# Reordered opening of the second attention of a four-layer kernel

## The chip, the cores and the metric

The kernel runs on one core of a Trainium2 chip. The metric is the device time of one execution in microseconds (us); the median of three executions of the kernel before is 891.05 us (890.66 to 892.91). A difference of 0.3% is 2.7 us.

## What is computed

The program is a chain of four layers; each has a gated cross-attention block and a gated feed-forward block. x and ctx are 8 x 128 x 256, taken as 1024 rows of 256 numbers. The change lies in the attention of the second layer ("attention 2" here): 16 heads of 16 numbers, queries, keys and values rounded to 8-bit steps, softmax, weights rounded to 255 steps:

```python
q = (x @ Wq + bq).reshape(1, B * N, H, hd)          # x is layer-normalised
kv = (cond @ Wkv + bkv).reshape(1, -1, 2, H, hd)
k, v = (kv[:, :, 0], kv[:, :, 1])
...
q = _fq_sym(q, axis=-1)
k = _fq_sym(k, axis=-1)
v = _fq_sym(v, axis=2)
attn = jnp.einsum('bhqd,bhkd->bhqk', q, k)
attn = jax.nn.softmax(attn.astype(jnp.float32), axis=-1)
attn = _fq_unsigned(attn, axis=-1)
out = jnp.einsum('bhqk,bhkd->bhqd', attn, v)
```

## The kernel before

Each engine runs one program, written out by hand in order; engines meet only at semaphores. A wait holds up everything behind it on its engine. The 1024 rows are 8 tiles of 128. Keys and values of attention 2 depend on ctx alone and are projected and rounded during the feed-forward block ahead of it, so that at the opening the rounded keys ka2 lie ready. The opening then goes like this:

- TensorE (PE) turns the rounded values (16 bf16 transposes, line 1222, into banks 0 and 1). ScalarE (ACT) copies them to v2 (two copies, line 1320).
- VectorE (DVE) finishes the residual sum (line 1026, from banks 4 to 7) and the layer norm, in two halves of four tiles: variance (line 159, semaphore var_ready), square root on ACT (`root`, line 1316, semaphore std_ready, in ACT's order behind the copies of v2), four short steps (lines 166 to 169), then the normalised rows xn tile by tile (line 171). PE turns them (line 214, f32), ACT copies them to xnT (`evacuate_T`, line 204).
- `project(half)` (line 1203) multiplies four tiles of xnT by wq2: 16 f32 matmuls of 128x256, two tiles to a bank. DVE's chain on the queries of a half goes from `take2` (line 1370, one instruction for a bank) over the scales to the rounded queries qa2, whose last instruction is line 1424 (semaphore qa2_ready).
- `turn_pairs` (line 1214) turns keys and queries, by pairs of heads: pairs 0 to 7 are keys, 8 to 15 queries. A pair is 8 bf16 transposes, one for each tile, into one of banks 4 to 7 in turn, so pair n waits for the copy of pair n - 4. ACT copies a key pair whole (line 1309, 128x1024) and the lower 64 rows of a query pair (line 1311, 64x1024); DVE copies the upper 64 rows of each query pair (line 1429) and the lower ones of pair 12 (line 1431).
- PE's order is: values, ln_tensor(2) with project(0) between the two halves, key pairs 0 to 3, project(1), key pairs 4 to 7, then a wait for both halves of qa2, then the query pairs, then a wait for the last copy.
- The loop of attention 2 follows: 128 steps n, one for each head and tile. PE makes the scores (line 1242, two matmuls of 128x512, three slots of two banks: n = 0 in banks 0 and 1, n = 1 in 2 and 3, n = 2 in 4 and 5), DVE takes the row maxima (`top`, line 1438), ACT the exponential (`exp`, line 1332), GpSimd rounds (line 1153), a DMA or PE turns the weights, and PE multiplies by the values seven steps later (lines 1263 and 1264). DVE too waits for the last copied pair ahead of its first `top`.

DMAs of this stretch are issued by SyncE (SP), which at the opening waits for the turned values and for the first 8 pairs (qkT2_blocks, line 1597), and then for the loop.

Of the kernel before, what the change touches and what calls it, by code (L numbers as in the profile page):

```python
# [46 lines left out]
def build(nc, A, out):  # L47
# [3 lines left out]
    def sem(name):  # L51
        if name not in sems:
            sems[name] = ctx.enter_context(nc.semaphore(name))
        return sems[name]
# [4 lines left out]
    with ctx:  # L59
# [1042 lines left out]
        def bf(i):  # L1102
            return bank[i].bitcast(BF16)
# [63 lines left out]
            sp.dma_start_transpose(rT2[n % RSLOTS2].rearrange("p (j q) -> p j q", j=NT), r2[n % RSLOTS2])\  # L1167
              .then_inc(sem(f"rT2_ready{n % RSLOTS2}"), 16)

        def low_by_vector(n):  # L1170
            return n == H2 // 2 + 4

        def pair_copied(eng, n):

            eng.wait_ge(sem("qkT2_ready"), sum(not low_by_vector(m) for m in range(n + 1)))
            if n >= H2 // 2:
                eng.wait_ge(sem("qT2_ready"), sum(1 + low_by_vector(m) for m in range(H2 // 2, n + 1)))

        def l1x_values_tensor(pe):

# [16 lines left out]
        def l1x_tensor(pe):  # L1197
# [7 lines left out]
                    if t % 2:  # L1205
                        last.then_inc(sem("qk2_done"), 1)

            def turn_pairs(numbers):

                for n in numbers:  # L1210
                    if n >= 4:
                        pair_copied(pe, n - 4)
                    for t in range(NT):
                        last = nc.tensor.transpose(bf(4 + n % 4)[:, t * P:(t + 1) * P],
                                                   (ka2 if n < H2 // 2 else qa2)[:, t, 2 * (n % 8):2 * (n % 8) + 2, :].rearrange("p a b -> p (a b)"),
                                                   identb[:])
                    last.then_inc(sem("qkT2_blocks"), 1)

            pe.wait_ge(sem("vi2_ready"), 1)
            for t in range(NT):  # L1220
                for c in range(DC):
                    last = nc.tensor.transpose(bf(t // 4)[:, (t % 4 * DC + c) * P:(t % 4 * DC + c + 1) * P],
                                               vi2[:, c, t * P:(t + 1) * P], identb[:])
                if t % 4 == 3:
                    last.then_inc(sem("v2_blocks"), 1)
            pe.wait_ge(sem("v2_ready"), 2)
            ln_tensor(pe, 2, lambda: project(0))
            pe.wait_ge(sem("ka2_ready"), 1)
            turn_pairs(range(4))
            project(1)  # L1230
            turn_pairs(range(4, H2 // 2))
            pe.wait_ge(sem("qa2_ready"), 2)
            turn_pairs(range(H2 // 2, H2))
            pe.wait_ge(sem("pads2_ready"), 32)
            pair_copied(pe, H2 - 1)

            def scores(n):
                h, t = n // NT, n % NT
                if n >= SRING2:
                    pe.wait_ge(sem("e2_ready"), n - SRING2 + 1)  # L1240
                for half in range(2):
                    last = nc.tensor.matmul(bank[2 * (n % SRING2) + half], qz2[:, h % 2, h // 2, t * P:(t + 1) * P],  # L1242
                                            kT2[:, h // 2, half * 512:(half + 1) * 512], start=True, stop=True)
                last.then_inc(sem("scores2_done"), 1)
# [55 lines left out]
                           kf2.rearrange("p t (h d) -> p (t h) d", h=H2)).then_inc(sem("ka2_high"), 1)  # L1300

        def l1x_scalar(act):
            def copy_pairs(numbers):
                for n in numbers:
                    if low_by_vector(n):
                        continue
                    act.wait_ge(sem("qkT2_blocks"), n + 1)
                    if n < H2 // 2:
                        nc.scalar.copy(kT2[:, n, :], bf(4 + n % 4)).then_inc(sem("qkT2_ready"), 1)
                    else:  # L1310
                        nc.scalar.copy(qz2[0:ROWS, 0, n % 8, :], bf(4 + n % 4)[0:ROWS]).then_inc(sem("qkT2_ready"), 1)

            def root(part):
                lo, hi = ln_parts(2)[part]
                act.wait_ge(sem("var_ready"), ln_roots(2) + part + 1)
                nc.scalar.activation(std[:, lo:hi], var_eps[:, lo:hi], ACT.Sqrt).then_inc(sem("std_ready"), 1)

            for b in range(2):
                act.wait_ge(sem("v2_blocks"), b + 1)
                nc.scalar.copy(v2[:, 4 * b:4 * b + 4, :].rearrange("p t d -> p (t d)"), bf(b)).then_inc(sem("v2_ready"), 1)  # L1320
            root(0)
            evacuate_T(act, xnT, sem("xnT_blocks"), sem("xnT_ready"), turned(2), 0)
            root(1)
            evacuate_T(act, xnT, sem("xnT_blocks"), sem("xnT_ready"), turned(2), 1)
            copy_pairs(range(H2))

            def exp(n):
                h, t = n // NT, n % NT
                act.wait_ge(sem("bias2_ready"), n + 1)
                if n >= ESLOTS2:  # L1330
                    act.wait_ge(sem("r2_ready"), n - ESLOTS2 + 1)
                nc.scalar.activation(e2[:, n % ESLOTS2, :], scores_at(n), ACT.Exp, bias=bias2[:, n:n + 1],  # L1332
                                     scale=s2[:, t * H2 + h:t * H2 + h + 1], accum_out=zs2[:, h, t:t + 1]).then_inc(sem("e2_ready"), 1)

            def copy_T(n):
# [12 lines left out]
            for half in range(2):  # L1348
                for c in range(DC):
                    act.wait_ge(sem("oT2_blocks"), 2 * half + c + 1)  # L1350
                    nc.scalar.activation(oT2[:, c, half * 512:(half + 1) * 512], bank[2 * half + c], ACT.Copy,
                                         scale=sv2[:, c:c + 1]).then_inc(sem("oT2_ready"), 1)
# [60 lines left out]
        def l1x_vector(dve, seq):  # L1413
            ln_vector(dve, seq, 2)
            for half in range(2):
# [7 lines left out]
                seq.step(round2(qf.rearrange("p t (h d) -> p (t h) d", h=H2), qa[:, :, 0:HD2]))  # L1423
                nc.vector.tensor_copy(qa[:, :, HD2:ROWS].rearrange("p n (a d) -> p n a d", a=3), bcast(qa[:, :, 0:HD2], 2, 3))\
                  .then_inc(sem("qa2_ready"), 1)
            for n in range(H2):
                if n >= H2 // 2:
                    dve.wait_ge(sem("qkT2_blocks"), n + 1)
                    nc.vector.tensor_copy(qz2[ROWS:P, 1, n % 8, :], bf(4 + n % 4)[ROWS:P]).then_inc(sem("qT2_ready"), 1)
                    if low_by_vector(n):  # L1430
                        nc.vector.tensor_copy(qz2[0:ROWS, 0, n % 8, :], bf(4 + n % 4)[0:ROWS]).then_inc(sem("qT2_ready"), 1)

            def top(n):
                h, t = n // NT, n % NT
# [27 lines left out]
                    dve.wait_ge(sem("values2_done"), n - RSLOTS2 + 1)  # L1462
                nc.vector.tensor_copy(rT2[n % RSLOTS2], bank[7].bitcast(F16)).then_inc(sem("rT2_copied"), 1)

            pair_copied(dve, H2 - 1)
            dve.wait_ge(sem("vi2_ready"), 1)
            U = H2 * NT
            for n in range(U):
# [1159 lines left out]
```

## Time and profile before

| | before |
|---|---|
| median of three | 891.05 us (890.66 to 892.91) |
| profiled execution | 892.17 us |
| its span, first to last instruction | 890.4 us |
| PE busy | 714.0 us, 80% |
| DVE busy | 534.0 us, 60% |
| ACT busy | 368.7 us, 41% |
| opening: last value transposes to the first `top` | 201.4 to 237.0 us |
| loop: first to last `top` | 237.0 to about 414 us |

All positions are microseconds from the start of the span. About 1.8 us of the time lie outside the span. In a row of the timeline the first number is the start, the second the length of the run of instructions merged into the row (x16 are sixteen of them), and the square bracket is the time for which the engine stood idle ahead of it and what ended that. PEclk is the granted clock of TensorE as a share of 2.4 GHz; it has two levels, 1.00 and 0.50 (1.2 GHz).

### The profile page before, as it was taken

How to read it: one execution, taken by the hardware profiler on the slowest of the kernel's cores; microseconds unless marked ns; L12 is line 12 of the kernel's file. 1: busy time of each engine (PE TensorE's matmuls, PEld its weight loads, DVE VectorE, ACT ScalarE, POOL GpSimd, SP SyncE). 2: the span in 40 equal slices, each digit the busy share in tenths (PEclk: the TensorE clock that was granted, in tenths of full speed). 3: DMA queues.
4: the chain of work that ended last, by engine and by line, in shares of the span. 5: the costliest groups of instructions: out<-in, count | busy, mean ns of one | idle time of the engine just before them, and what ended most of it. 6: DMA issues, size and time to landing. Idle time of an engine off the chain costs nothing.

```text
span 890.4 us, 14503 instructions
## 1 busy us (share of the span) xinstructions
PE 714.0 (80%) x5356; PEld 501.8 (56%) x5356; DVE 534.0 (60%) x1244; ACT 368.7 (41%) x658; POOL 303.3 (34%) x332
## 2 busy tenths in 40 slices
PE   5987798997588788887889980892966579999997
PEld 3445465676355555555657860471444446777776
DVE  3896855667899999996475545827776530000014
ACT  4002022424799999996222323342663122221210
POOL 2941130000277777775007506300320072000024
PEclk9997899997899999897898995796898569999999
DMA  7311174520199999999204848000013132515413
GB/s 239 132 59 48 26 148 159 197 74 1 23 176 193 161 198 169 183 174 161 102 25 118 146 126 279 10 0 1 0 54 137 47 87 91 207 48 182 160 39 118
DMA packets 139133, 100.08 MB, mean 112 GB/s; under 512 B 109204, under 2 KB 125238, under 8 KB 137016
## 3 DMA queue, kind: packets, MB, share of 16 engines
q1 hardware_dynamic: 132552, 81.19, 37.8%
q0 software_dynamic: 6224, 17.96, 7.6%
q8 instruction: 43, 0.70, 0.3%
q14 instruction: 26, 0.21, 0.1%
q10 hardware_dynamic: 288, 0.00, 0.0%
HBM read 61.15 MB, written 10.72 MB: 81 GB/s over the span
## 4 chain that ended last, share of the span: by engine, by line
PE 34%; issue 11%; DVE 10%; POOL 4%; ACT 4%; DMA 3%; POOLq 0%; DVEq 0%; ACTq 0%
PE psum L2342 7%; PE psum L2361 5%; PE psum L1661 3%; PE psum L1938 2%; PE psum L214 2%; ACT both L1332 2%; POOL both L568 2%; PE psum L1676 1%; DVE xnT L1438 1%; PE psum L1242 1%; PE psum L2372 1%; PE psum L1520 1%; DMA both<-both 1%; PE psum L621 1%; PE psum L635 1%
## 5 line engine op out<-in xcount | busy, mean ns | idle before, releaser
L1153 POOL TENSOR_SCALAR both<-both 128x1024 f16<-128x1024 f32 x128 | 133.7, 1045 | 162.8 <-ACT both L1332 155.0
L1438 DVE TENSOR_SCALAR_CACHE_REDUCE xnT<-psum,both 128x1024 bf16<-128x1024 f32 x128 | 157.5, 1278 | 9.1 <-PE psum L1242 8.9
L1332 ACT ACTIVATE both<-psum,both 128x1024 f32<-128x1024 f32 x128 | 153.5, 1210 | 9.2 <-DVE xnT L1438 8.7
L1242 PE MATMUL psum<-both 128*128 128x512 bf16 x256 | 84.4, 415 | 32.2 <-ACT both L1332 28.0
L2342 PE MATMUL psum<-both 128*128 128x320 f32 x256 | 73.5, 441 | 3.8 <-ACT both L556 3.8
L1263 PEld LDWEIGHTS psum<-both 128*128 128x128 f16 x1024 | 63.3, 98 | 22.7 <-DMA both<-both 8.3
L2421 ACT ACTIVATE both<-psum 128x320 f32<-128x320 f32 x64 | 27.6, 437 | 110.0 <-PE psum L2342 92.1
L1263 PE MATMUL psum<-both 128*128 128x16 f16 x1024 | 67.7, 171 | 6.4 <-DMA both<-both 2.8
L1264 PE MATMUL psum<-both,minus_base 128*128 128x16 f16 x1024 | 66.5, 170 | 0.0
L1264 PEld LDWEIGHTS psum<-both,minus_base 128*128 128x128 f16 x1024 | 58.6, 98 | 10.8 <-issue 2.7
L2342 PEld LDWEIGHTS psum<-both 128*128 128x128 f32 x256 | 48.8, 194 | 24.1 <-issue 5.3
L2361 PE MATMUL psum<-both 128*128 128x256 f32 (+1 forms) x272 | 60.5, 381 | 0.6 <-issue 0.6
L2456 DVE COPY both<-psum 128x256 f32<-128x256 f32 x14 | 5.9, 424 | 88.6 <-PE psum L2361 88.6
L2361 PEld LDWEIGHTS psum<-both 128*128 128x128 f32 (+1 forms) x272 | 50.4, 187 | 10.5 <-issue 2.5
L214 PE MATMUL psum<-ident,xn 128*128 128x128 f32 x128 | 25.9, 376 | 34.2 <-DVE xn L171 33.3
L428 POOL DMA_INDIRECT both<-moe_xn_dram,moe_token_of x31 | 30.3, 977 | 52.6 <-DVE both L400 24.6
L214 PEld LDWEIGHTS psum<-ident,xn 128*128 128x128 f32 x128 | 21.5, 194 | 38.6 <-DVE xn L171 31.5
L428 POOL DMA_INDIRECT both<-grouped_xn_dram,grouped_token_of x31 | 29.4, 949 | 30.5 <-DVE grouped_token_of L398 21.3
L1242 PEld LDWEIGHTS psum<-both 128*128 128x128 bf16 x256 | 15.3, 98 | 42.1 <-ACT both L1332 39.0
L187 ACT ACTIVATE std<-var_eps 128x4 f32<-128x4 f32 (+1 forms) x10 | 2.1, 208 | 84.0 <-DVE var_eps L159 84.0
L286 POOL TENSOR_TENSOR both<-both 128x512 f32<-128x512 f32 x32 | 32.2, 1038 | 12.9 <-ACT both L258 9.6
L1661 PE MATMUL psum<-both 128*128 x124 | 33.5, 394 | 0.3 <-ACT both L1703 0.3
(379 smaller groups left out, 1460.5 us busy)
## 6 DMA issues: line engine op xcount, KB each, us to landing
both<-in_l_experts SPq DMA_DIRECT2D x50, 384.0 KB, 3.7
both<-in_l_experts SPq DMA_DIRECT2D x16, 1024.0 KB, 5.5
grouped_y_dram<-both SPq DMA_DIRECT2D x31, 128.0 KB
ctok<-in_ctx SPq DMA_DIRECT2D x2, 1024.0 KB, 7.5
both<-kpad_dram SPq DMA_DIRECT2D x1, 2048.0 KB, 8.0
moe_xn_dram<-xn POOLq DMA_DIRECT2D x4, 512.0 KB, 3.9
both<-bp SPq DMA_DIRECT2D x2, 1024.0 KB, 12.1
moe_y_dram<-both POOLq DMA_DIRECT2D x7, 256.0 KB, 3.1
```

What stands on the lines that cost most here:

```text
L214: last = nc.tensor.transpose(bank[2 * half + c][:, t * P:(t + 1) * P], src[:, half * 4 + t, c * P:(c + 1) * P], ident[:])
L286: nc.gpsimd.tensor_tensor(kv[:, h % KVS, c, :].rearrange("p (b j i) -> p b j i", b=NT, j=HD0), bcast(rows, 3, HD0), bcast(rows, 2, HD0), A ...
L428: nc.gpsimd.indirect_dma_start(out=self.rows[:, b, :], out_offset=None, in_=self.xn_dram[:, :], in_offset=bass.IndirectOffsetOnAxis(ap=sel ...
L1153: nc.gpsimd.tensor_scalar(r2[n % RSLOTS2], e2[:, n % ESLOTS2, :], 255.0, HALF_BASE, ALU.mult, ALU.add).then_inc(sem("r2_ready"), 1)
L1242: last = nc.tensor.matmul(bank[2 * (n % SRING2) + half], qz2[:, h % 2, h // 2, t * P:(t + 1) * P], kT2[:, h // 2, half * 512:(half + 1) * ...
L1263: nc.tensor.matmul(dst, rT2[n % RSLOTS2][:, j * P:(j + 1) * P], of_block, start=(j == 0), stop=False)
L1264: last = nc.tensor.matmul(dst, minus_base[:], of_block, start=False, stop=(j == NT - 1))
L1332: nc.scalar.activation(e2[:, n % ESLOTS2, :], scores_at(n), ACT.Exp, bias=bias2[:, n:n + 1], scale=s2[:, t * H2 + h:t * H2 + h + 1], accum ...
L1438: nc.vector.tensor_scalar(scaled2[n % 2], scores_at(n), ns2[:, t * H2 + h:t * H2 + h + 1], None, ALU.mult, ALU.min, accum_out=bias2[:, n:n ...
L1661: last = nc.tensor.matmul(bank[b % 2][:, 0:2 * P].rearrange("p (j n) -> p j n", j=2), xT3[:, b % 4, c, :], w[:, :, c, :], start=(c == 0), ...
L2342: last = nc.tensor.matmul(bank[f % 4][:, 0:C7], w7[:, i, c * FF7 + f * P:c * FF7 + (f + 1) * P], moe7.rowsT[:, c, e * C7:(e + 1) * C7], st ...
L2361: last = nc.tensor.matmul(bank[4 + j][0:JT7[j][1], 0:D], h7[:, e % 2, f, JT7[j][0]:JT7[j][0] + JT7[j][1]], w7[:, e % 2, DC * FF7 + f * D:D ...
```

## The change

Nothing is computed otherwise, and no DMA is added, removed or moved. What changes is order and grain:

1. ACT: `root(0)` stands in front of the two copies of v2.
2. PE: key pairs 0 and 1 are turned right behind the values, once var_ready tells that banks 4 and 5 are free; key pairs 2 and 3 are turned between the two halves of xn, in front of `project(0)`. Pairs 4 and 5 come ahead of `project(1)`, 6 and 7 behind it. ACT's copies follow: key pair 0 ahead of the first half of xnT, 1 to 3 behind `root(1)`.
3. Queries are turned and copied by halves of four tiles: 8 pairs of 4 transposes after qa2_ready 1, then 8 pairs after qa2_ready 2. Copies are 64x512 each, 32 in all: of half 0, ACT makes the 8 lower and the first 5 upper ones, DVE the last 3 upper ones (in its order behind its whole chain on the queries); of half 1, ACT makes 6 lower ones, DVE 8 upper and 2 lower ones (pairs 2 and 5).
4. The first two scores wait for pair 0 of half 0 alone, and the wait for everything stands at n = 2. DVE's wait ahead of its first `top` is gone.

```diff
+        PAIRS2 = H2 // 2
+        def low_by_vector(half, m):
+            return half == 1 and m in (2, 5)
+        def high_by_vector(half, m):
+            return half == 1 or m >= 5
...
             pe.wait_ge(sem("vi2_ready"), 1)
...
+            pe.wait_ge(sem("ka2_ready"), 1)
+            pe.wait_ge(sem("var_ready"), ln_roots(2) + 1)
+            turn_keys(range(2))
             pe.wait_ge(sem("v2_ready"), 2)
-            ln_tensor(pe, 2, lambda: project(0))
-            pe.wait_ge(sem("ka2_ready"), 1)
-            turn_pairs(range(4))
+            ln_tensor(pe, 2, between_halves)
+            turn_keys(range(4, 6))
             project(1)
-            turn_pairs(range(4, H2 // 2))
-            pe.wait_ge(sem("qa2_ready"), 2)
-            turn_pairs(range(H2 // 2, H2))
+            turn_keys(range(6, PAIRS2))
+            turn_queries(0)
+            turn_queries(1)
             pe.wait_ge(sem("pads2_ready"), 32)
-            pair_copied(pe, H2 - 1)
             def scores(n):
+                if n < 2:
+                    q_copied(pe, 0, 0)
+                elif n == 2:
+                    q_copied(pe, 1, PAIRS2 - 1)
...
+            def between_halves():
+                turn_keys(range(2, 4))
+                project(0)
...
+            def turn_queries(half):
+                pe.wait_ge(sem("qa2_ready"), half + 1)
+                for m in range(PAIRS2):
+                    if m >= 4:
+                        q_copied(pe, half, m - 4)
+                    elif half:
+                        q_copied(pe, 0, m + 4)
+                    else:
+                        key_copied(pe, m + 4)
+                    for t in range(4):
+                        last = nc.tensor.transpose(bf(4 + m % 4)[:, t * P:(t + 1) * P],
+                                                   qa2[:, 4 * half + t, 2 * m:2 * m + 2, :].rearrange("p a b -> p (a b)"), identb[:])
+                    last.then_inc(sem("qkT2_blocks"), 1)
...
+            root(0)
             for b in range(2):
                 act.wait_ge(sem("v2_blocks"), b + 1)
                 nc.scalar.copy(v2[:, 4 * b:4 * b + 4, :].rearrange("p t d -> p (t d)"), bf(b)).then_inc(sem("v2_ready"), 1)
-            root(0)
+            copy_keys(range(1))
             evacuate_T(act, xnT, sem("xnT_blocks"), sem("xnT_ready"), turned(2), 0)
             root(1)
+            copy_keys(range(1, 4))
             evacuate_T(act, xnT, sem("xnT_blocks"), sem("xnT_ready"), turned(2), 1)
-            copy_pairs(range(H2))
+            copy_keys(range(4, PAIRS2))
+            for half in range(2):
+                for m in range(PAIRS2):
+                    copy_queries(half, m)
...
-            pair_copied(dve, H2 - 1)
             dve.wait_ge(sem("vi2_ready"), 1)
```

## Rows read from the trace of the kernel before

**Rows 1.** The page: the span.
```profile
span 890.4 us, 14503 instructions
```

**Rows 2.** Timeline, ScalarE, 194.9 to 216.6 us (start, length, instruction, idle before).
```profile
200.96 1.93 ACT L1320 CAST both<-psum 128x1024 f16<-128x1024 bf16 x2 [4.85 <-PE psum L1222]
202.90 1.28 ACT L1316 ACT_TABLE_LOAD   x1
204.20 0.20 ACT L1316 ACTIVATE std<-var_eps 128x4 f32<-128x4 f32 x1
207.63 1.07 ACT L204 COPY xnT<-psum 128x512 f32<-128x512 f32 x2 [3.23 <-PE psum L214]
```

**Rows 3.** Timeline, VectorE, 199 to 240 us.
```profile
201.84 0.17 DVE L159 TENSOR_SCALAR var_eps<-mv 128x4 f32<-128x4 f32 x1
...
204.50 0.18 DVE L166 RECIPROCAL rstd<-std 128x4 f32<-128x4 f32 x1 [1.18 <-ACT std L1316]
...
215.56 0.69 DVE L1370 TENSOR_TENSOR both<-psum,bqk 128x512 f32<-128x512 f32 x1 [2.29 <-PE psum L1203]
...
221.65 1.28 DVE L1370 TENSOR_TENSOR both<-psum,bqk 128x512 f32<-128x512 f32 x2
...
227.45 0.96 DVE L1424 COPY both<-both 128x3072 bf16<-128x3072 bf16 x1
...
234.07 1.91 DVE L1429 COPY both<-psum 64x1024 bf16<-64x1024 bf16 x3
236.99 1.28 DVE L1438 TENSOR_SCALAR_CACHE_REDUCE xnT<-psum,both 128x1024 bf16<-128x1024 f32 x1 [1.02 <-PE psum L1242]
```

**Rows 4.** Timeline, TensorE's matmuls, 199 to 240 us.
```profile
205.87 1.94 PE L214 MATMUL psum<-ident,xn 128*128 128x128 f32 x8 [4.50 <-DVE xn L171]
208.75 6.76 PE L1203 MATMUL psum<-wq,xnT 128*128 128x256 f32 x16 [0.95 <-ACT xnT L204]
215.35 1.04 PE L214 MATMUL psum<-ident,xn 128*128 128x128 f32 x8
...
218.01 3.67 PE L1203 MATMUL psum<-wq,xnT 128*128 128x256 f32 x16
221.52 1.95 PE L1214 MATMUL psum<-identb,both 128*128 128x128 bf16 x32
228.47 5.40 PE L1214 MATMUL psum<-identb,both 128*128 128x128 bf16 x64 [5.00 <-DVE both L1424]
236.23 1.46 PE L1242 MATMUL psum<-both 128*128 128x512 bf16 x6 [2.36 <-DVE both L1429]
```

**Rows 5.** Busy time by stretch: PE, PEld, DVE, ACT, POOL, PEclk, DMA share, GB/s.
```profile
201.40:204.60 3.20, 0.00 (x0) 0.00 (x0) 1.96 (x8) 2.97 (x4) 0.00 (x0) 1.00 0.00 0
204.80:214.90 10.10, 8.09 (x23) 6.47 (x24) 6.38 (x25) 1.23 (x3) 0.00 (x0) 0.50 0.00 0
228.70:231.90 3.20, 3.20 (x33) 3.20 (x32) 2.08 (x3) 2.44 (x3) 0.00 (x0) 0.50 0.00 0
232.10:234.00 1.90, 1.77 (x31) 1.57 (x29) 1.87 (x3) 1.90 (x4) 0.00 (x0) 1.00 0.00 0
```

**Rows 6.** Timeline, ScalarE, 215 to 240 us.
```profile
222.17 3.76 ACT L1309 COPY both<-psum 128x1024 bf16<-128x1024 bf16 x4 [1.11 <-PE psum L1214]
229.46 6.46 ACT L1311 COPY both<-psum 64x1024 bf16<-64x1024 bf16 x7 [3.53 <-PE psum L1214]
235.94 1.28 ACT L1332 ACT_TABLE_LOAD   x1
238.32 1.20 ACT L1332 ACTIVATE both<-psum,both 128x1024 f32<-128x1024 f32 x1 [1.10 <-DVE xnT L1438]
```

**Rows 7.** Instruction groups by shape, whole run or opening (count, busy us, mean ns, idle before).
```profile
L204 ACT COPY xnT<-psum 128x512 f32<-128x512 f32 x4 | 2.1, 588 | 10.7 <-PE psum L214 10.7
L1429 DVE COPY both<-psum 64x1024 bf16<-64x1024 bf16 x8 | 5.3, 692 | 1.6 <-PE psum L1214 1.5
L1782 DVE COPY both<-psum 128x256 f32<-128x256 f32 x31 | 13.2, 424 | 0.5 <-PE psum L1676 0.3
```

More of the change, by code:

```diff
@@ L1168, in l1x_turn_sync, with q_by_vector, key_copied, q_copied @@
               .then_inc(sem(f"rT2_ready{n % RSLOTS2}"), 16)
[L1170 to L1177, printed above, removed]
+        PAIRS2 = H2 // 2
[3 more added lines that the diff above has]
+            return half == 1 or m >= 5
+        def q_by_vector(half, m):
+            return low_by_vector(half, m) + high_by_vector(half, m)
+        def key_copied(eng, n):
+            eng.wait_ge(sem("qkT2_ready"), n + 1)
+        def q_copied(eng, half, m):
+            done = [(a, b) for a in range(half + 1) for b in range(PAIRS2) if (a, b) <= (half, m)]
+            by_vector = sum(q_by_vector(a, b) for a, b in done)
+            eng.wait_ge(sem("qkT2_ready"), PAIRS2 + 2 * len(done) - by_vector)
+            if by_vector:
+                eng.wait_ge(sem("qT2_ready"), by_vector)
         def l1x_values_tensor(pe):
@@ L1206, in project, with turn_keys @@
                         last.then_inc(sem("qk2_done"), 1)
-            def turn_pairs(numbers):
+            def turn_keys(numbers):
                 for n in numbers:
                     if n >= 4:
-                        pair_copied(pe, n - 4)
+                        key_copied(pe, n - 4)
                     for t in range(NT):
                         last = nc.tensor.transpose(bf(4 + n % 4)[:, t * P:(t + 1) * P],
-                                                   (ka2 if n < H2 // 2 else qa2)[:, t, 2 * (n % 8):2 * (n % 8) + 2, :].rearrange("p a b -> p (a b)"),
-                                                   identb[:])
+                                                   ka2[:, t, 2 * n:2 * n + 2, :].rearrange("p a b -> p (a b)"), identb[:])
                     last.then_inc(sem("qkT2_blocks"), 1)
+            def turn_queries(half):
[14 more added lines that the diff above has]
+                project(0)
             pe.wait_ge(sem("vi2_ready"), 1)
@@ L1302, in l1x_scalar, with copy_keys, copy_queries @@
         def l1x_scalar(act):
-            def copy_pairs(numbers):
+            def copy_keys(numbers):
                 for n in numbers:
-                    if low_by_vector(n):
-                        continue
                     act.wait_ge(sem("qkT2_blocks"), n + 1)
[L1308 to L1311, printed above, removed]
+                    nc.scalar.copy(kT2[:, n, :], bf(4 + n % 4)).then_inc(sem("qkT2_ready"), 1)
+            def copy_queries(half, m):
+                some = slice(512 * half, 512 * (half + 1))
+                if q_by_vector(half, m) < 2:
+                    act.wait_ge(sem("qkT2_blocks"), PAIRS2 * (half + 1) + m + 1)
+                if not low_by_vector(half, m):
+                    nc.scalar.copy(qz2[0:ROWS, 0, m, some], bf(4 + m % 4)[0:ROWS, 0:512]).then_inc(sem("qkT2_ready"), 1)
+                if not high_by_vector(half, m):
+                    nc.scalar.copy(qz2[ROWS:P, 1, m, some], bf(4 + m % 4)[ROWS:P, 0:512]).then_inc(sem("qkT2_ready"), 1)
             def root(part):
@@ L1425, in l1x_vector @@
                   .then_inc(sem("qa2_ready"), 1)
[L1426 to L1431, printed above, removed]
+            for half in range(2):
+                for m in range(PAIRS2):
+                    some = slice(512 * half, 512 * (half + 1))
+                    if q_by_vector(half, m):
+                        dve.wait_ge(sem("qkT2_blocks"), PAIRS2 * (half + 1) + m + 1)
+                    if high_by_vector(half, m):
+                        nc.vector.tensor_copy(qz2[ROWS:P, 1, m, some], bf(4 + m % 4)[ROWS:P, 0:512]).then_inc(sem("qT2_ready"), 1)
+                    if low_by_vector(half, m):
+                        nc.vector.tensor_copy(qz2[0:ROWS, 0, m, some], bf(4 + m % 4)[0:ROWS, 0:512]).then_inc(sem("qT2_ready"), 1)
             def top(n):
```

## The prediction

> **What bounds the kernel now.** I read the timeline engine by engine from the last value transposes to the first step of the loop, because the change touches no other stretch, and then the granted clock of the same stretch. The span is 890.4 us [rows 1], the profiled execution took 892.17, so 1.8 us lie outside; everything below is subtracted from 892.17.
>
> The reader is to see one chain. The row of VectorE's line 166 waits for ScalarE's square root [rows 3]; that root stands behind two copies of the values and a table load, though its input was ready at 201.84 + 0.17 = 202.0 [rows 2, 3]. TensorE meanwhile stood idle for 4.50 us up to 205.87 [rows 4]. Its clock was still 1.00 in 201.4 to 204.6, in which it ran nothing, and 0.50 from 204.8 to 214.9 [rows 5]. So project(0) took 6.76 us, where project(1) took 3.67 at the full clock [rows 4]. VectorE's second take of half 0 waits for the end of project(0), at 215.56 [rows 3]. From there VectorE runs without a pause to the last query row at 227.45 + 0.96 = 228.4: half 1's take starts at 221.65, when half 0's chain ends [rows 3]. Only then are queries turned, from 228.47 [rows 4], and copied, to 234.07 + 1.91 = 236.0 [rows 3]. Scores follow at 236.23 [rows 4], the first top at 236.99 [rows 3], the first exponential at 238.32 [rows 6].
>
> **The change part by part.**
>
> Root first. ScalarE is free 4.85 us before 200.96, at 196.1 [rows 2]. A table load does not wait for the semaphore of the activation behind it: the one for the exponential ran at 235.94, and its exponential waited 1.10 us more for VectorE [rows 6]. So the square root's table load (1.28 us) goes into that idle time and the root ends at about 202.25. VectorE was free 1.18 us before 204.50, at 203.3 [rows 3], so line 166 starts at 203.37 and all behind it comes 1.13 us earlier. If the load did wait for var_ready, the root would end at 203.5 and the values' copies at 205.4, which holds up TensorE's first turned row by 0.7; that is the other bound. Queued behind the root's wait are the values' copies: they now run from 202.3 to 204.2, and the first xn is ready at about 204.7 (205.87 - 1.13), so that wait costs nothing.
>
> First keys ahead. A key pair is 8 transposes of 1.95/32 = 0.061 us [rows 4]. Pairs 0 and 1 take 1.0 us from 202.05; TensorE then idles from 203.05 to 204.74 instead of from 201.4 to 205.9. I cannot tell from the trace whether the clock falls in that gap, so I work out both.
> (a) It falls, as before, near 204.7. Eight row transposes take 1.94 us [rows 4], to 206.7; key pairs 2 and 3 follow without a gap, 16 transposes at about 0.107 (0.061 would be full clock), to 208.4. ScalarE's copies of xnT (1.07 us [rows 2]) end at 207.9, inside that. From 204.74 to 208.4 TensorE then has no pause; before, a run of bf16 transposes just as long and as dense, from 228.47 [rows 4], at 0.50 in 228.7 to 231.9, had the clock back at 1.00 by 232.1 [rows 5]. So I take it to be back when project(0) starts, at 208.4; project(0) takes 3.67 and ends at 212.05.
> (b) It does not fall. Rows end at about 206.1 (paced by VectorE's xn), copies at 207.3, project(0) at 211.0.
> Against 215.5 that is 3.5 us in (a), 4.5 in (b). Cover of key pairs 2 and 3: ScalarE's copy of xnT; in (a) they stick out by 0.5 us, which is counted.
>
> VectorE's chain on the queries keeps its length, 228.41 - 215.56 = 12.85 us, if project(1) is ready for half 1. In (a): half 1's rows are turned from 212.05 in 1.04 us [rows 4], copied by 214.2, key pairs 4 and 5 meanwhile, project(1) from 214.3 to 218.0; half 0's chain ends at 212.05 + 6.1 = 218.15. It holds, just. The chain ends at 224.9.
>
> Queries by halves. The grain doubles the copies: 32 of 64x512 for 16 of 64x1024. ScalarE: seven 64x1024 copies take 6.46 us, 0.92 each [rows 6]; two copies of 512 columns take 1.07 of which the last is 0.588 [rows 2, 7], so 0.48 from start to start. The trace has no 64x512 bf16 copy: 0.48 is the nearest row by columns, 0.92 the upper bound if width costs nothing. I take 0.48. VectorE: 0.692 for 1024 bf16 columns, 0.424 for 256 f32 columns [rows 7]; 1024 bf16 columns in about the time of 512 f32 ones, so 512 bf16 cost about 0.42 and, overlapped as in [rows 3] (three in 1.91, so 0.61 for 0.69), 0.34. Bounds 0.34 and 0.61.
> (a) Key pair 6 is turned behind project(1), at 218.5; its copy starts at 218.65, pair 7's copy lets ScalarE go at 220.5 (0.92 each [rows 6]). Then 13 copies of half 0 to 226.7 and 6 of half 1: 220.5 + 19 x 0.48 + 0.1 = 229.7. VectorE makes 13 copies from 224.9: 224.9 + 13 x 0.34 = 229.3, and 0.4 for pairs that TensorE turns late (a turn waits for both engines' copies four pairs ahead); 229.7. Both end together. Before, ScalarE alone had 6.5 us behind the chain's end; now 13 of its 19 query copies lie beside VectorE's half 1. The cover is gone if a copy costs more: ScalarE decides.
>
> Scores ahead. Slots 0 and 1 lie in banks 0 to 3, free by then, so scores 0 and 1 run right behind the last turn, from about 228.85. With the clock possibly down again (TensorE has little to do from 220 to 228) two matmuls take up to 0.86, so top(0) starts at 230.0, where before it waited 1.02 us for scores [rows 3]. The exponential's table load (229.7 to 231.0) ends before top(0) does (231.3).
>
> The new waits of TensorE (q_copied) hold up only its own next turns. SyncE's wait for the first 8 pairs is met by the keys, as before; no DMA moves. GpSimd waits for the first exponential alone.
>
> Sum in (a): 236.99 - 230.0 = 7.0 us: 3.5 from the chain's start, 3.5 from its end to top(0) (8.6 before, 5.1 after). In (b) the start is 1.0 earlier: 8.0. Nothing behind the first top changes, and all its waits are for events of the loop, so the gain is carried to the end, give or take where the clock falls in later stages. I take the middle, 7.5: 892.17 - 7.5 = **884.7 us**. The profiled execution is 1.1 above the median; project(0) ran nearly wholly at 0.50 in it, and another execution could get the clock back earlier, so I don't take that 1.1 off again; the low end allows for it.
>
> **The rivals.**
> Transposes don't raise the clock. Then project(0) starts cold at 208.4 and ends at 215.1; of the start's gain 0.4 is left, of the end's 3.5: 892.17 - 3.9 = 888.2. For it: in the stretch from 204.8 the clock came back only at the end, though row transposes and then project(0) ran in it [rows 4, 5]. Against it: 228.7 to 231.9 [rows 5]. The Trainium skill ("TensorE: Matmul & The Clock Gate", Part 4) says that transposes do not count as busy in the way matmuls do and that the full clock does not engage for them; by that rule this rival is the outcome. The trace disagrees: PE had only transposes before the clock went from 0.50 to 1.00.
>
> A copy costs by the instruction, not by its columns (the other side). ScalarE's 19 query copies at 0.92 to 1.02 each end 8.4 to 10.3 us later than at 0.48: 1.4 to 3.3 us slower than the 892.17, 893.6 to 895.5. It decides from 0.48 + 7.0/19 = 0.85 per copy on. Against it: 588 ns for 512 columns in f32 [rows 7].
>
> The gain is given back later: the loop or the stage behind it waits for something that does not move, and the time is 890 to 892. For it, only that ScalarE and VectorE fill the loop so evenly that a lost PE clock can show; I find no transfer that is issued at a fixed time.
>
> **How the numbers follow.** Forecast (cases a and b, with their bounds) 0.80; clock stays low 0.08 (888.2); gain given back 0.07; copies dear 0.05. With VectorE's copies at 0.61, 13 of them end 3.5 us later, and the forecast itself becomes 884.7 + 3.5 = 888.2, so the range goes from 882.6 (8.0 off, and the 1.1 of the median with 0.5 of later clock) to 888.6. The measurement can tell about 0.3%, 2.7 us. Faster by more than that than 891.05 are the forecast and most of the clock case: 0.85; within 0.3%: 0.10; slower: 0.05.
>
> **What would show it.** Right: square root at about 202, its table load near 196; first take of half 0 ahead of 211; project(0) near 3.7 us at clock 1.00; chain end near 225 (224 in b); ScalarE copying queries from 220 on without a pause; first top near 230. Wrong: project(0) above 5 us; a 64x512 copy on ScalarE above 0.7 us; VectorE waiting more than 1 us between its 13 copies; a first top after 233, or the loop longer than the 177 us from 237.0 to 414.

## The result and the profile after

The changed kernel took 885.77 us (median of 20, 882.47 to 890.85), the kernel before beside it 892.2 (median of 20, 887.37 to 896.14). The ratio is 0.9941, 95% interval 0.9924 to 0.9958, so about 5.3 us less (3.7 to 6.8); the two medians lie 6.4 us apart. 884.7 was forecast. The profiled execution of the changed kernel took 886.11 us with a span of 884.4.

I follow the opening by its length, from the first value transpose to the first top, since its start lies anywhere from 198.4 to 204.1 us in the profiles below: 237.0 - 200.3 = 36.7 us before, 231.45 - 200.76 = 30.7 after, so 6.0 us less.

ScalarE after (timeline, 194.9 to 236 us: start, length, instruction, idle before; line 1356 is the root, 1361 the values' copies, 1349 and 1351 the lower and upper query copies, 1377 the exponential):

```profile
196.58 1.28 ACT L1356 ACT_TABLE_LOAD   x1
202.50 0.20 ACT L1356 ACTIVATE std<-var_eps 128x4 f32<-128x4 f32 x1 [4.64 <-DVE var_eps L159]
202.61 1.91 ACT L1361 CAST both<-psum 128x1024 f16<-128x1024 bf16 x2
...
220.34 0.58 ACT L1349 COPY both<-psum 64x512 bf16<-64x512 bf16 x1
220.95 0.58 ACT L1351 COPY both<-psum 64x512 bf16<-64x512 bf16 x1
221.56 0.58 ACT L1349 COPY both<-psum 64x512 bf16<-64x512 bf16 x1
...
226.39 4.57 ACT L1349 COPY both<-psum 64x512 bf16<-64x512 bf16 x9
230.97 1.28 ACT L1377 ACT_TABLE_LOAD   x1
232.77 1.20 ACT L1377 ACTIVATE both<-psum,both 128x1024 f32<-128x1024 f32 x1 [0.52 <-DVE xnT L1486]
```

The table load sits in the idle time at 196.6 and the root runs as soon as the variance is there, ahead of the values' copies; compare [rows 2]. The row to look at twice is 220.34 and the ones below it: these ten copies, in turn on the lower and the upper 64 of the 128 partitions (called rows here, as in the change), start every 0.605 us, the nine in one row below, all on the lower ones, every 0.50.

TensorE after (timeline, 194.9 to 236; line 1227 turns keys, 1242 queries, 1216 is project, 1278 the scores), and its clock (columns as in [rows 5]):

```profile
202.62 1.05 PE L1227 MATMUL psum<-identb,both 128*128 128x128 bf16 x16 [0.79 <-DVE var_eps L159]
205.18 1.67 PE L214 MATMUL psum<-ident,xn 128*128 128x128 f32 x8 [1.51 <-DVE xn L171]
206.64 1.91 PE L1227 MATMUL psum<-identb,both 128*128 128x128 bf16 x16
208.35 4.05 PE L1216 MATMUL psum<-wq,xnT 128*128 128x256 f32 x16
...
226.51 3.58 PE L1242 MATMUL psum<-identb,both 128*128 128x128 bf16 x32 [0.69 <-ACT both L1351]
230.13 0.81 PE L1278 MATMUL psum<-both 128*128 128x512 bf16 x3
```
```profile
201.90:205.60 3.70, 1.48 (x20) 1.30 (x20) 3.49 (x15) 2.93 (x4) 0.00 (x0) 1.00 0.00 0
205.80:209.00 3.20, 3.20 (x23) 3.02 (x23) 2.73 (x14) 2.11 (x5) 0.00 (x0) 0.50 0.00 0
209.20:219.20 10.00, 9.84 (x79) 8.72 (x77) 8.30 (x16) 5.27 (x7) 0.00 (x0) 1.00 0.01 2
```

The gap of 4.50 us in [rows 4] is two pieces of 0.79 and 1.51. The clock still fell, but TensorE then ran row and key transposes without a pause and had the clock back 0.8 us into project(0), which took 4.05 us for 6.76.

VectorE after (timeline, 199 to 236; 1415 is the take, 1469 the last query row, 1477 the upper query copies, 1486 the top):

```profile
203.81 0.18 DVE L166 RECIPROCAL rstd<-std 128x4 f32<-128x4 f32 x1
212.44 0.69 DVE L1415 TENSOR_TENSOR both<-psum,bqk 128x512 f32<-128x512 f32 x1 [1.03 <-PE psum L1216]
...
224.34 0.96 DVE L1469 COPY both<-both 128x3072 bf16<-128x3072 bf16 x1
225.33 1.11 DVE L1477 COPY both<-psum 64x512 bf16<-64x512 bf16 x3
227.13 1.45 DVE L1477 COPY both<-psum 64x512 bf16<-64x512 bf16 x3 [0.69 <-PE psum L1242]
...
231.45 1.28 DVE L1486 TENSOR_SCALAR_CACHE_REDUCE xnT<-psum,both 128x1024 bf16<-128x1024 f32 x1
```

Line 166 waits for nothing now, and the top follows the last copy at once, where [rows 3] has 1.18 and 1.02 us of idle time. The new wait is 0.69 us ahead of half 1's first copy: VectorE waits for a turn, and the turn for ScalarE's copies (TensorE's row at 226.51).

### The profile page after: what moved, and what is told of

Same layout as the page of the kernel before. It is cut to its first block, busy times and chain, and to the rows that moved or that the text cites. A ratio compares the mean times of both kernels' runs of the same rounds, so it can differ in the third digit from the quotient of the medians.

```text
span 884.4 us, 14478 instructions
## 1 busy us (share of the span) xinstructions
PE 703.4 (80%) x5311; PEld 497.6 (56%) x5356; DVE 534.9 (60%) x1248; ACT 373.0 (42%) x670; POOL 304.4 (34%) x332
## 4 chain that ended last, share of the span: by engine, by line
PE 46%; DVE 22%; issue 18%; ACT 6%; POOL 4%; DMA 4%; POOLq 0%; DVEq 0%; SPq 0%; ACTq 0%
PE psum L2389 7%; PE psum L2408 6%; PE psum L1708 3%; PE psum L879 3%; DVE xnT L1486 3%; DVE both L329 2%; PE psum L214 2%; DVE both L333 2%; PE psum L635 2%; ACT both L1377 2%; PE psum L1278 2%; PE psum L1985 2%; DVE stats L142 2%; POOL both L568 2%; PE psum L1723 2%
## 5 line engine op out<-in xcount | busy, mean ns | idle before, releaser
L1278 PE MATMUL psum<-both 128*128 128x512 bf16 x215 | 76.7, 426 | 40.7 <-ACT both L1377 37.7
L214 PEld LDWEIGHTS psum<-ident,xn 128*128 128x128 f32 x128 | 19.5, 182 | 39.0 <-DVE xn L171 34.0
```

Source lines behind the costliest of these rows:

```text
L214: last = nc.tensor.transpose(bank[2 * half + c][:, t * P:(t + 1) * P], src[:, half * 4 + t, c * P:(c + 1) * P], ident[:])
```

## The experiments

Each is one profile and, where a ratio stands, six to ten times, that of the profile among them. Single times scatter by 2.5 us about their mean, so the ratios can tell only large parts; openings are read from the profiles. An opening must be compared at the same behaviour of the clock in the gap ahead of the rows, which fell in some executions and stayed up in others; I say which.

**The root behind the values' copies again** (changed kernel, ScalarE):
```diff
-            root(0)
             for b in range(2):
                 act.wait_ge(sem("v2_blocks"), b + 1)
...
+            root(0)
```


> The changed kernel with only the square root put back behind the two copies of the values on ScalarE. I measure the opening from the first value transpose to the first top: 36.7 us in the profile before, 30.7 in the one after. My theory: the root in front is worth what VectorE waited for it, 1.1 us, and everything behind is in series with it: opening 31.8. Rival: the start is covered, because TensorE has key pairs 2 and 3 to turn and project(0) waits for them anyhow: opening 30.7.


Measured: opening 229.8 - 198.4 = 31.4 us, clock fallen as in the changed kernel; ratio 0.9962 (0.9931 to 0.9993). Line 166 came 1.14 us later, but only 0.7 us arrived at the end, because project(0), starting later, found the clock back already (3.67 us). So the rival falls: the root is worth 0.7 us here. How the clock came back in this profile is shown further down.

**The root alone, on the kernel before.**
```diff
+            root(0)
             for b in range(2):
                 act.wait_ge(sem("v2_blocks"), b + 1)
...
-            root(0)
```


> The kernel before with only the square root moved in front of the values' copies. My theory: VectorE's line 166 starts 1.14 us earlier, at 3.05 after the first value transpose instead of 4.19, and project(0) starts 1.1 earlier but cold, as before: opening 34 to 35.6 us. Rival: the earlier start is given back, because project(0) only spends longer at the lower clock: opening as in the kernel before, 36.0 to 36.7.


Measured: one time, 892.33 us, which tells nothing by itself. In the profile line 166 starts 3.05 us after the first value transpose instead of 4.19, project(0) takes 5.71 us and the opening is 34.9, for 36.7 and 36.1 in the two profiles of the kernel before. So the root carries through there, too: 1.2 us against the profile whose project(0) took nearly as long (5.87), and 1.8 against the other.

**No keys ahead at all** (changed kernel, TensorE and ScalarE):
```diff
-            turn_keys(range(2))
             pe.wait_ge(sem("v2_ready"), 2)
-            ln_tensor(pe, 2, between_halves)
-            turn_keys(range(4, 6))
+            ln_tensor(pe, 2, lambda: project(0))
+            turn_keys(range(4))
             project(1)
-            turn_keys(range(6, PAIRS2))
+            turn_keys(range(4, PAIRS2))
...
-            copy_keys(range(1))
-            copy_keys(range(1, 4))
-            copy_keys(range(4, PAIRS2))
+            copy_keys(range(PAIRS2))
...
```


> The changed kernel with all keys turned and copied where they were before (0 to 3 behind the rows, 4 to 7 behind project(1), ScalarE's eight copies behind the second half of xnT); root first, queries by halves and early scores stay. My theory: with no transposes ahead of it TensorE stands idle for over 3 us, the clock falls, and project(0) takes 5.5 to 6.8 us; moreover ScalarE's copies of keys 4 to 7 come behind project(1) and push its 19 query copies back: opening (first value transpose to first top) 34 to 36 us, so nearly all of the 6.0 us is gone. Rival (the gain is the root's and the halves'; keys are only displaced): opening 30.7 to 31.5.


Measured: ratio 1.0002 (0.997 to 1.0034), opening 34.25 us, clock fallen. TensorE (timeline) and ScalarE's key copies (timeline):
```profile
204.42 1.94 PE L214 MATMUL psum<-ident,xn 128*128 128x128 f32 x8 [3.36 <-DVE xn L171]
207.31 5.55 PE L1216 MATMUL psum<-wq,xnT 128*128 128x256 f32 x16 [0.95 <-ACT xnT L204]
```
```profile
219.51 3.76 ACT L1340 COPY both<-psum 128x1024 bf16<-128x1024 bf16 x4 [1.11 <-PE psum L1227]
```
Both prices of the theory are there: project(0) at 5.55 us, and four key copies behind project(1), in front of the query copies. The keys carry the larger part of the change: of 6.0 us, 3.6 are gone without them, though not nearly all, as was expected. Of the 3.6, VectorE's last query row comes 1.2 later (25.75 us after the first value transpose for 24.54), and 2.35 are lost behind it (8.50 us from there to the first top for 6.15). So the place of the key copies on ScalarE costs more here than the slower project(0). This is the one experiment whose ratio lies clear of the changed kernel's.

**Keys between the halves, but none ahead of the rows** (changed kernel; pairs 0 and 1 between, 2 to 5 ahead of project(1)).
```diff
-            turn_keys(range(2))
...
             def between_halves():
-                turn_keys(range(2, 4))
+                turn_keys(range(2))
                 project(0)
...
-            turn_keys(range(4, 6))
+            turn_keys(range(2, 6))
...
```
ScalarE's key copies move along.


> The changed kernel with no keys ahead of the rows: key pairs 0 and 1 are turned between the two halves of the rows, in front of project(0), and pairs 2 to 5 ahead of project(1). TensorE's idle gap ahead of the rows is whole again, so the clock falls. My theory: row transposes and the 16 key transposes, dense, bring it back about when project(0) starts: project(0) about 4 us, opening 31 to 31.5. Rival (transposes don't raise the clock): project(0) about 6.5 us and opening 33 to 34.


Measured: ratio 0.9941 (0.9914 to 0.9967), opening 31.35 us. TensorE (timeline) and its clock (by stretch):
```profile
204.84 1.31 PE L214 MATMUL psum<-ident,xn 128*128 128x128 f32 x8 [3.36 <-DVE xn L171]
206.00 1.77 PE L1227 MATMUL psum<-identb,both 128*128 128x128 bf16 x16
207.56 4.65 PE L1216 MATMUL psum<-wq,xnT 128*128 128x256 f32 x16
```
```profile
206.20:209.40 3.20, 3.20 (x21) 2.84 (x19) 2.72 (x15) 2.73 (x5) 0.00 (x0) 0.50 0.00 0
209.60:212.00 2.40, 2.40 (x12) 2.09 (x12) 1.14 (x3) 0.05 (x1) 0.00 (x0) 1.00 0.00 0
```
The clock fell only at about 206.1 and was back by 209.6, after transposes and a short piece of project(0). 4.65 us lies nearer to the theory's 4 than to 6.5. It is no pure case, since project(0) ran 2 us of that stretch itself; the pure ones are in [rows 5] and in the profile shown under "Clock" below.

**Keys ahead of the rows, but none between the halves** (changed kernel).
```diff
             def between_halves():
-                turn_keys(range(2, 4))
                 project(0)
...
-            turn_keys(range(4, 6))
+            turn_keys(range(2, 6))
...
```
ScalarE's key copies move along.


> The changed kernel with key pairs 2 and 3 turned behind the second half of the rows, so that project(0) follows the first half's copy directly, after a pause of TensorE of about 1 us. My theory: the turned keys keep TensorE dense and so bring the clock back; without them project(0) starts 0.6 us earlier but runs at 0.50 for longer, takes 5 to 6.5 us instead of 4.05, and the opening is 31.5 to 32.5 instead of 30.7. Rival (transposes don't raise the clock, the keys only stand in the way): project(0) takes about 4 and the opening is 30.1 to 30.7.


Measured: ratio 0.9969 (0.9946 to 0.9992). The clock never fell in this execution: project(0) started 6.8 us after the first value transpose, took 3.72, opening 30.1. The theory's 31.5 to 32.5 did not come, and the rival's numbers did, but both spoke of a clock that had fallen, so the profile can't tell the two apart. Something else shows: the scores experiment below had the clock up too and the same last query row (23.4 us after the first value transpose in both), and its last copy ended 0.5 us earlier. What differs is project(1), which ends 0.5 us later here because keys stand in front of it, and with it ScalarE's copies of keys 6 and 7. So ScalarE decided the end.

**Queries in whole pairs again** (the kernel before with root and keys moved; TensorE's order of keys and projections is the changed one, its queries and scores are as before).
```diff
...
-            root(0)
+            copy_pairs(range(1))
             evacuate_T(act, xnT, sem("xnT_blocks"), sem("xnT_ready"), turned(2), 0)
             root(1)
+            copy_pairs(range(1, 4))
             evacuate_T(act, xnT, sem("xnT_blocks"), sem("xnT_ready"), turned(2), 1)
-            copy_pairs(range(H2))
+            copy_pairs(range(4, H2))
```


> The kernel before with the root and the keys moved as in the change, but the queries still turned and copied in whole pairs behind both halves, and all scores behind the last copy. My theory: the start keeps its gain (first take's end 3.1 us earlier), the end gets its old 8.6 us from VectorE's last query row to the first top back, for 6.15 in the changed kernel: opening 30.7 + 2.4 = 33.1. Rival: the end's gain is nil, since ScalarE's 19 copies cost as much as 7 long ones: opening 30.7.


Measured: ratio 0.994 (0.9911 to 0.997), opening 32.5 us with the clock up. VectorE (timeline):
```profile
222.93 0.96 DVE L1432 COPY both<-both 128x3072 bf16<-128x3072 bf16 x1
225.01 0.69 DVE L1437 COPY both<-psum 64x1024 bf16<-64x1024 bf16 x1 [1.13 <-PE psum L1214]
...
229.87 1.91 DVE L1437 COPY both<-psum 64x1024 bf16<-64x1024 bf16 x3
232.96 1.28 DVE L1446 TENSOR_SCALAR_CACHE_REDUCE xnT<-psum,both 128x1024 bf16<-128x1024 f32 x1 [1.19 <-PE psum L1248]
```
From the last query row to the first top it takes 232.96 - 223.89 = 9.1 us; the changed kernel takes 231.45 - 225.30 = 6.15. The halves and early scores are worth 2.4 to 2.9 in the opening. The ratio is the changed kernel's own and doesn't show that loss; its interval is too wide to deny it. A part of it comes back in the loop, which took 176.0 us here and 177.5 and 177.1 in the two profiles of the changed kernel (see below): opening and loop together are 208.5 us against 208.1 and 207.7, though the clock that stayed up had brought this profile's last query row 1.1 us ahead. So the halves and early scores shorten the opening, but that they shorten the time is not shown.

**All scores behind the last copy again** (changed kernel).
```diff
-                if n < 2:
-                    q_copied(pe, 0, 0)
-                elif n == 2:
+                if n == 0:
                     q_copied(pe, 1, PAIRS2 - 1)
...
+            q_copied(dve, 1, PAIRS2 - 1)
             dve.wait_ge(sem("vi2_ready"), 1)
```


> The changed kernel with all scores, and VectorE's first top, again behind the last copied query. My theory: VectorE's wait for the first scores comes back, 0.8 to 1.0 us: opening 31.5 to 31.7. Rival: the exponential's table load and ScalarE's last copies end so late that the first exponential starts at the same point, 32.0 us after the first value transpose, and only the first top moves.


Measured: ratio 0.9952 (0.9928 to 0.9976), opening 30.8 us with the clock up. VectorE and ScalarE (timelines):
```profile
230.03 0.77 DVE L1475 COPY both<-psum 64x512 bf16<-64x512 bf16 x2
232.12 1.28 DVE L1484 TENSOR_SCALAR_CACHE_REDUCE xnT<-psum,both 128x1024 bf16<-128x1024 f32 x1 [1.32 <-PE psum L1276]
```
```profile
230.49 1.28 ACT L1375 ACT_TABLE_LOAD   x1
233.45 1.20 ACT L1375 ACTIVATE both<-psum,both 128x1024 f32<-128x1024 f32 x1 [1.68 <-DVE xnT L1484]
```
The wait is back, 1.32 us. The first exponential starts 32.2 us after the first value transpose, close to the rival's 32.0, but that figure was for a clock that fell; ScalarE stands idle for 1.68 us ahead of it and waits for VectorE's top, not for its own copies or table load, so the rival's reason falls. The wait is more than the 0.8 to 1.0 expected; the first scores ran with TensorE's clock at 0.50 (granted in 230.9 to 232.1).

**ScalarE's first ten query copies in another order** (changed kernel: lower, upper, upper, lower, ...).
```diff
-                if not low_by_vector(half, m):
...
-                if not high_by_vector(half, m):
...
+                for upper in (1, 0) if half == 0 and m % 2 else (0, 1):
+                    if not upper and not low_by_vector(half, m):
...
+                    if upper and not high_by_vector(half, m):
...
```


> The changed kernel with ScalarE's first ten query copies in another order: lower, upper, upper, lower and so on, instead of lower, upper, lower, upper. In the changed kernel these ten started every 0.605 us, the nine lower ones behind them every 0.50. My theory: a copy on the same 64 rows as the one before overlaps it by some 0.1 us, one on the other rows does not: starts 0.50 after a copy on the same rows, 0.605 after one on the other, 0.4 us less in all, and the first top 0.4 earlier. Rival (VectorE's or TensorE's traffic at that time slows all copies): 0.605 throughout the ten.


Measured: ratio 0.9936 (0.9906 to 0.9966), opening 30.0 us, clock fallen. ScalarE (timeline):
```profile
221.12 0.58 ACT L1350 COPY both<-psum 64x512 bf16<-64x512 bf16 x1
221.73 1.06 ACT L1352 COPY both<-psum 64x512 bf16<-64x512 bf16 x2
222.82 1.06 ACT L1350 COPY both<-psum 64x512 bf16<-64x512 bf16 x2
```
Two copies on the same 64 rows take 1.06 us, so the second starts 0.48 after the first; a copy on the other 64 rows starts 0.605 after. The ten take 5.56 us (221.12 to 226.68) for 6.05. VectorE and TensorE did the same work beside them: the theory holds, the rival falls. The opening is 0.7 us shorter than in the changed kernel: 0.2 came from a project(0) that ran wholly at 1.00, 0.5 from VectorE's wait for its first turn of half 1, which fell from 0.69 to 0.21 us.

**Keys 6 and 7 ahead of project(1), with that order** (changed kernel).
```diff
-            turn_keys(range(4, 6))
+            turn_keys(range(4, PAIRS2))
             project(1)
-            turn_keys(range(6, PAIRS2))
```


> The same order of copies, and key pairs 6 and 7 turned ahead of project(1) as well. My theory: ScalarE's 19 query copies end the opening, and they wait for the copies of keys 6 and 7, which wait for project(1). With those two copied during project(1), the query copies start 1.1 us earlier, right after half 0 of the queries is ready; project(1) ends 0.9 later, which VectorE's take of half 1 just covers. Opening 29.0 to 29.5 with the clock fallen in the gap (30.7 in the changed kernel), 28.0 to 28.5 without; time 1.5 us below the changed kernel. Rival: VectorE's 13 copies or project(1)'s later end decide: opening 30.5 or more.


Measured: 885.16 us (median of 8), ratio 0.9916 (0.9885 to 0.9947), opening 29.5 us with the clock fallen, at the upper end of what was expected; the median lies 0.6 us below the changed kernel's, less than the 1.5 expected and within the scatter. VectorE (timeline; 1477 copies upper rows, 1479 lower ones):
```profile
226.68 2.13 DVE L1477 COPY both<-psum 64x512 bf16<-64x512 bf16 x6
228.84 0.42 DVE L1479 COPY both<-psum 64x512 bf16<-64x512 bf16 x1
229.29 1.11 DVE L1477 COPY both<-psum 64x512 bf16<-64x512 bf16 x3
```
VectorE now copies without a pause from 226.68 to the first top at 231.68: ScalarE no longer ends the opening. VectorE too pays for a change of rows: six copies on the same rows take 2.13 us, so they start 0.34 apart, while the lower copy starts 0.45 after the last upper one, and the next upper one 0.45 after it.

**One copy less on VectorE** (the version above, pair 5's lower copy of half 1 on ScalarE).
```diff
-            return half == 1 and m in (2, 5)
+            return half == 1 and m == 2
```


> The version with keys 6 and 7 ahead of project(1) and the other order of copies, and pair 5's lower copy of half 1 moved from VectorE to ScalarE. There VectorE copied without a pause for 5.0 us up to the first top while ScalarE waited for turns, so VectorE ended the opening. My theory: 12 copies on VectorE, 0.36 us less: opening 29.1 with the clock fallen in the gap, 28.0 without. Rival: ScalarE, now with 20 copies and the exponential's table load behind them, ends it: first top 0.36 earlier, first exponential not.


Measured: 883.99 us (median of 6), ratio 0.9908 (0.9879 to 0.9937), opening 28.2 us with the clock up. The exponential starts right behind the first top, so ScalarE's table load doesn't end it. VectorE's copies no longer do either (timeline):
```profile
228.62 1.28 DVE L1486 TENSOR_SCALAR_CACHE_REDUCE xnT<-psum,both 128x1024 bf16<-128x1024 f32 x1 [0.36 <-PE psum L1277]
```
The first top now waits 0.36 us for TensorE's scores, and from the last query row to the first top 0.24 us are gained (5.04 to 4.80) where 0.36 was expected. It is the shortest opening of all; its ratio lies below the changed kernel's, but the intervals overlap, so that it is faster in time is not shown.

**Second profiles of the kernel before and of the changed kernel**, both without an edit.


> The kernel before once more, for a second profile of its opening. My theory: project(0) never gets the clock back before it starts, so it takes 5 to 6.8 us in any execution (6.76 in the first profile) and the opening, from the first value transpose to the first top, 35 to 36.7 us. Rival: 6.76 was an accident of that execution, project(0) can take under 4.5 and the opening is then 34.5 or less, so that most of the start's gain is one execution's.

> The changed kernel once more. Two of its relatives (scores put back, keys 2 and 3 behind the rows) kept the clock at 1.00 over the gap ahead of the rows. If this execution keeps it too: project(0) 3.7, ends 10.5 after the first value transpose, opening 29.5. If the clock falls: 30.0 to 30.7 as in the first profile. Rival: the two relatives kept it because of their edits and the changed kernel itself never does.


Measured: project(0) 5.87 us and opening 36.1 before; 3.82 and 30.6 after, clock fallen. TensorE in the kernel before (timeline):
```profile
205.86 1.77 PE L214 MATMUL psum<-ident,xn 128*128 128x128 f32 x8 [4.49 <-DVE xn L171]
208.57 5.87 PE L1203 MATMUL psum<-wq,xnT 128*128 128x256 f32 x16 [0.95 <-ACT xnT L204]
```
So 6.76 was on the high side, not an accident, and the second pair gains 5.5 us. The rival on the changed kernel stands: the clock fell in both of its profiles.

## Why the prediction was right, step by step

**Root first: right.** The load of the square root's table ran in ScalarE's idle time, and line 166 moved from 4.19 to 3.05 us after the first value transpose, the 1.13 forecast.

**Clock: right, as case (a), with two errors that cancel.** The transposes brought it back, and the rival that they don't falls. In the changed kernel the stretch at 0.50 holds row and key transposes and only 0.7 us of project(0), and 1.00 follows. In the profile with the root behind the values' copies nothing but transposes ran between the fall and the rise (TensorE, timeline; then its clock by stretch):
```profile
203.94 1.94 PE L214 MATMUL psum<-ident,xn 128*128 128x128 f32 x8 [2.65 <-DVE xn L171]
205.67 1.56 PE L1227 MATMUL psum<-identb,both 128*128 128x128 bf16 x16
207.07 3.67 PE L1216 MATMUL psum<-wq,xnT 128*128 128x256 f32 x16
```
```profile
203.40:206.40 3.00, 2.46 (x15) 2.43 (x16) 2.96 (x12) 0.70 (x2) 0.00 (x0) 0.50 0.00 0
206.80:207.00 0.20, 0.20 (x7) 0.20 (x5) 0.04 (x1) 0.20 (x2) 0.00 (x0) 1.00 0.00 0
```
The Trainium skill ("TensorE: Matmul & The Clock Gate", Part 4) states that the full clock does not engage for transposes; these rows disagree with it.

In the changed kernel the clock came back 0.8 us into project(0), not just ahead of it, which cost 0.4 us. But project(0) started 7.6 us after the first value transpose where 208.4 - 200.3 = 8.1 was forecast, because the clock fell only between 205.6 and 205.8, while the first rows were being turned. So project(0) ended at 11.6, the 212.05 - 200.3 = 11.7 forecast; that these two cancel is luck. Case (b), clock up throughout, came in four of the nine profiles with two key pairs ahead of the rows and in none of the five without. Neither profile of the changed kernel itself is among the four, and nine and five are too few to show that the keys keep the clock up.

**VectorE's chain: right.** 212.44 to 225.30 is 12.86 us, forecast 12.85; with the start's gain, its end came 3.6 us earlier, forecast 3.5. The 3.5 was measured from a project(0) of 6.76 us, the longest of all; in the second pair, with 5.87 before, the chain's end came 2.6 us earlier.

**Queries by halves: the term that was mis-sized.** ScalarE's 19 copies were put at 0.48 us from start to start, 9.2 in all. They took 10.6 (220.34 to 230.96): ten alternate between lower and upper rows and start 0.605 apart. The 0.48 had come from two copies on the same rows [rows 2, 7]; the order experiment shows that this was the choice that failed. VectorE's price, 0.34, was right for copies on the same rows (three in 1.11), but its 13 copies took 6.1 us for the 4.8 forecast. Of that, 0.69 is the wait for a turn that waited for ScalarE, where 0.4 was forecast; and the ten copies of half 1 took 4.29 us for some 3.5, since four of them change rows, 0.1 us more each, and the first three took 1.45 for 1.11. Together: from last query row to first top 6.15 us, forecast 5.1.

**Scores ahead: right.** The top follows the last copy within 0.03 us; 0.3 was forecast.

The sum for the opening is 6.0 us where (a) said 7.0, and the missing 1.0 is the end's. The other order of ScalarE's copies brings back 0.5 of it, and keys 6 and 7 ahead of project(1) 0.6 more (6.15, 5.67 and 5.04 us from last query row to first top). In the second pair the 5.5 us are 2.6 from the start and 2.9 from the end.

**"The gain is carried to the end": not quite, and open why.** The loop from first to last top (instruction by line; start of the first and of the last one), before, before again, after, after again:
```profile
L1438 DVE TENSOR_SCALAR_CACHE_REDUCE xnT<-psum,both x128: 1177/1278/1285, 237.0 to 413.0; 128x1024 bf16<-128x1024 f32 x128
```
```profile
L1438 DVE TENSOR_SCALAR_CACHE_REDUCE xnT<-psum,both x128: 1178/1280/1285, 236.4 to 412.6; 128x1024 bf16<-128x1024 f32 x128
```
```profile
L1486 DVE TENSOR_SCALAR_CACHE_REDUCE xnT<-psum,both x128: 1177/1279/1286, 231.4 to 408.9; 128x1024 bf16<-128x1024 f32 x128
```
```profile
L1486 DVE TENSOR_SCALAR_CACHE_REDUCE xnT<-psum,both x128: 1177/1279/1286, 230.4 to 407.5; 128x1024 bf16<-128x1024 f32 x128
```
176.0 and 176.2 us against 177.5 and 177.1: 1.5 and 0.9 us given back. The prediction had named a loop longer than the 177 us from 237.0 to 414 as a sign of being wrong, and that sign came: counted like that, to the end of the last top, the first pair has 177.2 before and 178.7 after. The mean clock of the loop goes along, two views by stretch, before and after:
```profile
237.00:413.00 176.00, 141.36 (x2426) 95.45 (x2424) 167.91 (x279) 166.83 (x268) 130.48 (x125) 0.91 1.02 174
```
```profile
231.40:408.90 177.50, 135.12 (x2383) 95.73 (x2424) 167.35 (x280) 168.34 (x267) 130.44 (x125) 0.89 1.03 172
```
The experiment without keys between the halves had 175.3 us and a clock of 0.91, so a short opening doesn't have to bring a long loop. An earlier start alone doesn't bring it either: the experiment with queries in whole pairs starts its loop at 233.0 and has 176.0 us and 0.91. All four profiles with whole query pairs have 176.0 to 176.2 us (both of the kernel before, the root alone, whole pairs again); of the ten with halves, nine are longer, 176.4 to 177.5. That points at the halves and early scores, but whether they make the clock fall more often in the loop, or these executions happened to, no run here separates.

**The time.** 884.7 was forecast and 885.77 measured, which is closer than the terms are. The 7.5 was the middle of (a) and (b). The clock fell in both profiles of the changed kernel, so (a)'s 7.0 is to be compared: 6.0 and 5.5 came in the opening, and the loop gave 1.5 and 0.9 back. That leaves 4.5 and 4.6, inside the 3.7 to 6.8 of the ratio. The profiled times agree with the opening's 6.0 (892.17 - 886.11 = 6.1) only by luck: the changed kernel's opening began 0.45 us later, and the part behind the loop, which the change doesn't touch, took 475.5 us for 477.4. Not taking the 1.1 us of the median off again fits the 892.2 of these 20 times, but the kernel before had medians of 891.54 and 890.64 in two other sets of 31, so that, too, is partly luck.

## What to carry to other kernels

Work that needs nothing from a waiting chain can pay twice when it moves ahead. The key transposes fill TensorE's idle time ahead of the costly matmuls, and project(0) took 3.67 to 4.65 us with them and 5.55 to 6.76 without; and their copies no longer stand in front of the query copies on ScalarE, which was worth more (2.35 of 3.6 us). When work is cut into smaller copies, price them by measured rows in which the partitions change from one copy to the next as they will there, not only by rows of the same size, and look for the copy that all others wait behind, here two key copies behind project(1). Where the clock differs from one execution to the next, compare stretches of profiles at the same clock, since times that scatter by 2.5 us can't tell parts of 1 us.

## What was not expected of the hardware

A ScalarE copy out of PSUM starts 0.48 to 0.50 us after the one before if both are on the same 64 rows, 0.605 us if the rows change (64x512 bf16, 0.58 us each). On VectorE the same copies (0.42 us each) start 0.34 and 0.45 us apart. Transposes alone took the granted clock from 0.50 to 1.00. And with one burst of sixteen transposes in the gap of 3.4 to 4.5 us ahead of the rows the clock stayed at 1.00 in four profiles of nine, without it in none of five; whether the burst is the cause is open.
